# Expert rows weighted by a gate and added in memory into one row per token

## The reference, cut to what matters

```python
x = L0_attn_x                                  # 4 x 2048 x 256, so N = 8192 tokens
x = x + recurrence(layernorm(x)) * silu(ffn0(layernorm(x)))        # layer 0
xn = layernorm(x)
x = x + attention(xn) * silu(experts(xn))      # layer 1

def experts(xt):                               # E = 8, K = 2, capacity 2048
    logits = xt @ wg
    topv, topi = top_k(softmax(logits), K)
    topv = topv / sum(topv)                    # the gate
    pos, valid = place of each (token, choice) in its expert's queue, pos < capacity
    disp[topi, pos] += xt                      # rows of an expert
    y = relu(disp @ w1 + b1) @ w2 + b2         # per expert, 2048 rows
    return sum over k of gate * valid * y[topi, pos]
```

## Time and profile before

| | us |
|---|---|
| median of 3 runs | 1557.62 (1556.9 to 1558.34) |
| the profiled execution | 1556.35 |
| its span | 1554.5 |
| TensorE, VectorE busy | 1274.6, 1005.9 |
| ScalarE, GpSimd busy | 601.1, 577.3 |
| `recur` | 252.8 to 321.6 |
| `attend` | 321.6 to 659.6 |
| `route` | 659.6 to 714.6 |
| `experts` | 714.6 to 1461.75 |
| `combine` | 1461.75 to 1554.5 |

### The profile page before, as it was taken

How to read it: one execution, slowest core, us unless ns; L and a number is a source line. 1 busy time by engine, 2 the same in 40 slices (tenths; PEclk the granted TensorE clock), 3 DMA queues, 4 the chain that set the end, 5 groups by cost and what they waited for, 6 DMA issues and landing times. The chain is left out here.

```text
span 1554.5 us, 22804 instructions
## 1 busy us (share of the span) xinstructions
PE 1274.6 (82%) x7727; PEld 877.9 (56%) x7727; DVE 1005.9 (65%) x1760; ACT 601.1 (39%) x883; POOL 577.3 (37%) x540
## 2 busy tenths in 40 slices
PE   2999997769899988345999999999999999999200
PEld 1656653338777777223766666677567656766200
DVE  2788873047999999697655556555555655565297
ACT  0555553212222222102455344544544454454263
POOL 2122220003666666702333433434343333433245
PEclk9999997669999999655999999999999999999655
DMA  8000004500000000012213131221313122222596
GB/s 299 1 0 0 0 0 198 235 28 26 29 27 27 27 27 28 2 53 61 69 41 110 52 97 48 77 72 47 105 55 97 52 75 72 78 66 52 144 316 215
DMA packets 70758, 116.84 MB, mean 75 GB/s; under 512 B 6449, under 2 KB 57523, under 8 KB 68496
## 3 DMA queue, kind: packets, MB, share of 16 engines
q1 hardware_dynamic: 51456, 74.38, 14.0%
q0 software_dynamic: 12720, 33.96, 7.2%
q10 hardware_dynamic: 6496, 7.36, 1.4%
HBM read 66.13 MB, written 50.33 MB: 75 GB/s over the span
## 5 line engine op out<-in xcount | busy, mean ns | idle before, releaser
L1558 ACT ACTIVATE e_h_all<-e_pH,e_b1c,e_h_scale 128x512 f32<-128x512 f32 x256 | 199.7, 780 | 369.2 <-PE e_pH L1605 367.0
L1624 PE MATMUL e_pY<-e_w_hi,e_h_hi 128*128 128x256 f16 x1024 | 279.3, 273 | 5.0 <-DVE e_w_lo L1469 5.0
L1626 PE MATMUL e_pY<-e_w_hi,e_h_lo 128*128 128x256 f16 x1024 | 279.1, 273 | 0.0
L1625 PE MATMUL e_pY<-e_w_lo,e_h_hi 128*128 128x256 f16 x1024 | 279.1, 273 | 0.0
L1384 POOL DMA_INDIRECT e_xg<-xn_rows,e_icol x136 | 153.4, 1128 | 300.2 <-DVE e_icol L1410 258.4
L1497 DVE TENSOR_TENSOR e_h_lo<-e_h_all,e_h_hi 128x512 f16<-128x512 f32 x256 | 177.3, 693 | 107.6 <-ACT e_h_hi L1558 96.2
L1603 PE MATMUL e_pH<-e_x_hi,e_w_hi 128*128 128x512 f16 x512 | 196.4, 384 | 9.0 <-issue 6.4
L1604 PE MATMUL e_pH<-e_x_lo,e_w_hi 128*128 128x512 f16 x512 | 196.3, 383 | 0.0
L1605 PE MATMUL e_pH<-e_x_hi,e_w_lo 128*128 128x512 f16 x512 | 196.2, 383 | 0.0
L1396 POOL DMA_INDIRECT expert_rows<-e_yo,e_dcol x128 | 130.2, 1018 | 153.4 <-DVE e_yo L1521 122.4
L1521 DVE SCALAR_TENSOR_TENSOR e_yo<-e_pY,e_y_scale,logit_st 128x1024 f32<-128x1024 f32 x32 | 41.1, 1284 | 154.4 <-PE e_pY L1626 149.3
(11 more groups left out here) (226 smaller groups left out, 2293.8 us busy)
## 6 DMA issues: line engine op xcount, KB each, us to landing
raw<-expert_w SPq DMA_DIRECT2D x18, 1024.0 KB
expert_rows<-r_zero SPq DMA_DIRECT2D x16, 1024.0 KB, 15.8
xn_rows<-c_xn SPq DMA_DIRECT2D x16, 512.0 KB, 2.9
f_ya<-expert_rows SPq DMA_DIRECT2D x16, 512.0 KB, 5.2
f_yb<-expert_rows SPq DMA_DIRECT2D x16, 512.0 KB, 6.1
out<-f_ya SPq DMA_DIRECT2D x16, 512.0 KB, 3.5
x_st<-x ACTq DMA_DIRECT2D x4, 1536.0 KB, 13.9
e_xg<-xn_rows,e_icol POOLq DMA_INDIRECT x136
```

The costliest lines, as they stand in the source:

```text
L1558: last = act.activation(dst, pH[h % NPH][:, :], ACT.Relu, bias=b1c[eu][:, h:h + 1], scale=h_scale[eu][:, 0:1])
L1624: pe.matmul(pY[:, q, :], h_hi[:, h, cols], w2_hi[:, h, :], start=(h == 0), stop=False)
L1625: pe.matmul(pY[:, q, :], h_hi[:, h, cols], w2_lo[:, h, :], start=False, stop=False)
L1626: last = pe.matmul(pY[:, q, :], h_lo[:, h, cols], w2_hi[:, h, :], start=False, stop=(h == HT - 1))
```

## The change

The two rows that a token gets from its experts are weighted where they are made and added up in memory, so that the last stage reads one row per token.

- `xn_rows` gets eight more columns, the token's logits. ScalarE stores them in `attend`, one DMA per tile, at the head of the loop body (L982 of the changed file).
- The gather brings these columns along with the row. VectorE forms, after the lower half of x, the largest of the other experts' logits less this expert's own (`margin`: add a mask with -3e38 in this expert's column, maximum, subtract), ScalarE takes Exp of it, and after `yo` VectorE adds 1, takes the reciprocal, which is the gate, and multiplies the 128x1024 `yo` by it. GpSimd's scatter waits for that product.
- The scatter adds to memory (`compute_op=ALU.add`), into `expert_sums` of 8192 + 2048 rows, the last 2048 for empty places. At the end of an expert GpSimd waits until its scatters have landed, since the next expert may add to the same rows. GpSimd's loop now has four groups per iteration instead of two.
- `recur` fills 10240 instead of 16384 rows with zeros. `route` no longer makes the gates; the constants are longer by a mask and the row numbers of empty places.
- `combine` has one load, silu, product, addition and store per tile.
- In `attend` three small buffers became one, to make room; the operations are the same.

```diff
-    v.xn3_dram = nc.dram_tensor("xn3_rows", [N, D], F32, kind="Internal").ap()
-    v.y_dram = nc.dram_tensor("expert_rows", [TOPK * N, D], F32, kind="Internal").ap()
+    v.xn3_dram = nc.dram_tensor("xn3_rows", [N, D + E], F32, kind="Internal").ap()
+    v.y_dram = nc.dram_tensor("expert_sums", [N + CAP, D], F32, kind="Internal").ap()
...
-                parts = TOPK * N // (P * 8)
+                parts = (N + CAP) // (P * 8)
...
+                def store_logits(t):
+                    act.wait_ge(l_evac, t + 2)
+                    act.dma_start(rows[t][:, :, D:], v.logit_st[:, :, t, :]).then_inc(lg_out, 16)
...
-                dve.wait_ge(e_out, 1)
-                linked(dve.tensor_scalar(ep[:, :], ee[:, :], 1.0, None, ALU.add))
-                linked(dve.reciprocal(gates[:, 0, :], ep[:, :]))
-                linked(dve.tensor_tensor(gates[:, 1, :], ee[:, :], gates[:, 0, :], ALU.mult))
...
-                        pool.wait_ge(yb_ready, 2 * i + u + 1 + 1)
+                        pool.wait_ge(weighted, n + 1)
                         pool.sem_inc(passed, 1)
                         for q in range(BLK):
                             pool.indirect_dma_start(
                                 v.y_dram, bass.IndirectOffsetOnAxis(dcol[u][:, q:q + 1], axis=0), yo[u][:, q, :], None,
-                                bounds_check=TOPK * N - 1, oob_is_err=False).then_inc(y_out[u], 16)
+                                bounds_check=N + CAP - 1, oob_is_err=True, compute_op=ALU.add).then_inc(y_out[u], 16)
+                        if g == GRPS - 1:
+                            for m in range(2):
+                                pool.wait_ge(y_out[m], 8 * BLK * GRPS * (e + 1) + 16 * m)
...
+                def margin(n, u, e, first=1):
+
+                    dve.tensor_tensor(rest[:, :, :], xg[u][:, :, D:D + E], v.cst[:, C_X:C_X + (E + 1) * E][:, bass.ts(e, E)]
+                                      .unsqueeze(1).broadcast_to([P, BLK, E]), ALU.add).then_inc(gate_step, 1)
+                    dve.wait_ge(gate_step, first)
+                    dve.tensor_reduce(over[:, :], rest[:, :, :], AX.X, ALU.max).then_inc(gate_step, 1)
+                    dve.wait_ge(gate_step, first + 1)
+                    dve.tensor_tensor(gate[u][:, :], over[:, :], xg[u][:, :, D:][:, :, bass.ds(e, 1)]
+                                      .rearrange("p q o -> p (q o)"), ALU.subtract).then_inc(gate_in, 1)
...
                     x_lower(n + 1)
+                    margin(n + 1, 1 - u, e + (g + 1) // GRPS, 4 * n + 3)
                     take_icol(n + 2, u)
...
+                    dve.wait_ge(gate_out, n + 1)
+                    dve.tensor_scalar(gate[u][:, :], gate[u][:, :], 3e38, 1.0, ALU.min, ALU.add).then_inc(gate_step, 1)
+                    dve.wait_ge(gate_step, 4 * n + 5)
+                    dve.reciprocal(gate[u][:, :], gate[u][:, :]).then_inc(gate_step, 1)
+                    dve.wait_ge(gate_step, 4 * n + 6)
+                    dve.sem_inc(passed, 1)
+                    dve.wait_ge(yb_ready, n + 2)
+                    dve.tensor_tensor(yo[u][:, :, :], yo[u][:, :, :],
+                                      gate[u][:, :].unsqueeze(2).broadcast_to([P, BLK, D]),
+                                      ALU.mult).then_inc(weighted, 1)
...
                     x_upper(n + 1)
+                    margin_exp(n + 1, 1 - u)
...
-                    for k, y in enumerate((ya[n], yb[n])):
-                        sp.dma_start(y[:, :].rearrange("p (b d) -> p b d", b=B), rows[t, k]).then_inc(y_in[n], 16)
+                    sp.dma_start(ya[n][:, :].rearrange("p (b d) -> p b d", b=B), rows[t]).then_inc(y_in[n], 16)
```

More of the change, by code:

```diff
@@ L63 @@
 C_G = C_E + E
-C_ALL = C_G + TOPK * NG
+C_D = C_G + TOPK * NG
+C_X = C_D + P
+C_ALL = C_X + (E + 1) * E
 def constants():
@@ L76, in constants @@
     c[:, C_E:C_E + E] = np.arange(E)
-    c[:, C_G:] = np.ldexp(np.arange(P)[:, None] + float(P), np.arange(TOPK * NG)[None, :] - CODE)
+    c[:, C_G:C_D] = np.ldexp(np.arange(P)[:, None] + float(P), np.arange(TOPK * NG)[None, :] - CODE)
+    c[:, C_X:C_X + E * E] = np.where(np.eye(E), -3e38, 0.0).reshape(-1)
+    c[:, C_D:C_X] = N + np.arange(P)[:, None] + P * (np.arange(P) % (CAP // P))
     return c
@@ L820, in _ @@
                         sp.wait_ge(xn_ready, t + 1)
-                        sp.dma_start(rows[t], xn[u][:, :, :]).then_inc(xn_out[u], 16)
+                        sp.dma_start(rows[t][:, :, 0:D], xn[u][:, :, :]).then_inc(xn_out[u], 16)
                 for u in range(2):
                     sp.wait_ge(xn_out[u], 16 * NT // 2 + 16)
+                sp.wait_ge(lg_out, 16 * NT)
             @block.gpsimd
@@ L1291, in experts @@
         dcol = [sb(f"e_dcol{n}", [P, BLK], I32) for n in range(2)]
-        xg = [sb(f"e_xg{n}", [P, BLK, D]) for n in range(2)]
+        rest = sb("e_rest", [P, BLK, E])
+        over = sb("e_over", [P, BLK])
+        gate = [sb(f"e_gate{n}", [P, BLK]) for n in range(2)]
+        xg = [sb(f"e_xg{n}", [P, BLK, D + E + 1]) for n in range(2)]
         x_hi = sb("e_x_hi", [P, KD, W], F16)
@@ L1329, in experts @@
         y_out = [sem(f"e_y_out{n}") for n in range(2)]
+        gate_step = sem("e_gate_step")
+        gate_in = sem("e_gate_in")
+        gate_out = sem("e_gate_out")
+        weighted = sem("e_weighted")
         NGR = E * GRPS
@@ L1389, in _ @@
                     gather(u, u)
-                with pool.Fori(0, NGR // 2) as i:
-                    for u in range(2):
-                        gather(2 * i + u + 2, u)
-                        pool.wait_ge(yb_ready, 2 * i + u + 1 + 1)
+                with pool.Fori(0, E) as e:
+                    for g in range(GRPS):
+                        u = g % 2
+                        n = GRPS * e + g
+                        gather(n + 2, u)
+                        pool.wait_ge(weighted, n + 1)
                         pool.sem_inc(passed, 1)
@@ L1486, in _ @@
                 x_lower(0)
+                margin(0, 0, 0)
                 def body(e, eu, g, n):
@@ L1546, in _, with margin_exp @@
                 upper_w1(0, 0)
+                def margin_exp(n, u):
+                    act.wait_ge(gate_in, n + 1)
+                    act.sem_inc(passed, 1)
+                    act.activation(gate[u][:, :], gate[u][:, :], ACT.Exp).then_inc(gate_out, 1)
                 x_upper(0)
+                margin_exp(0, 0)
                 def body(e, eu, g, n):
@@ L1644, in combine @@
         ya = [sb(f"f_ya{n}", [P, B * D]) for n in range(NB)]
-        yb = [sb(f"f_yb{n}", [P, B * D]) for n in range(NB)]
         y_in = [sem(f"f_y_in{n}") for n in range(NB)]
         passed = sem("f_passed")
-        first_ready = sem("f_first_ready")
-        sum_ready = sem("f_sum_ready")
         silu_ready = sem("f_silu_ready")
@@ L1690, in _, with body @@
                     sp.wait_ge(o_out[n], 16 * (NT // NB) + 16)
+            @block.scalar
+            def _(act):
+                def body(i, n, left):
+                    act.wait_ge(y_in[n], 16 * (i + 1))
+                    act.sem_inc(passed, 1)
+                    act.activation(ya[n][:, :], ya[n][:, :], ACT.Silu).then_inc(silu_ready, 1)
+                rounds(act, body)
             @block.vector
             def _(dve):
-                def add(i, n):
-                    t = NB * i + n
-                    dve.wait_ge(y_in[n], 32 * (i + 1))
-                    dve.wait_ge(first_ready, t + 1)
-                    for b in range(B):
-                        cols = slice(b * D, (b + 1) * D)
-                        last = dve.scalar_tensor_tensor(ya[n][:, cols], yb[n][:, cols],
-                                                        v.gates[:, 1, bass.ds(b * NT + t, 1)], ya[n][:, cols],
-                                                        ALU.mult, ALU.add)
-                    last.then_inc(sum_ready, 1)
-                add(0, 0)
-                add(0, 1)
                 def body(i, n, left):
                     t = NB * i + n
-                    if left >= 2:
-                        add(i + (n + 2) // NB, (n + 2) % NB)
                     dve.wait_ge(silu_ready, t + 1)
@@ L1725, in _ @@
                 rounds(pool, body)
-            @block.scalar
-            def _(act):
-                def silu(t, n):
-                    act.wait_ge(sum_ready, t + 1)
-                    act.activation(ya[n][:, :], ya[n][:, :], ACT.Silu).then_inc(silu_ready, 1)
-                def first(i, n):
-                    t = NB * i + n
-                    act.wait_ge(y_in[n], 32 * (i + 1))
-                    act.sem_inc(passed, 1)
-                    for b in range(B):
-                        cols = slice(b * D, (b + 1) * D)
-                        last = act.activation(ya[n][:, cols], ya[n][:, cols], ACT.Copy,
-                                              scale=v.gates[:, 0, bass.ds(b * NT + t, 1)])
-                    last.then_inc(first_ready, 1)
-                first(0, 0)
-                first(0, 1)
-                first(0, 2)
```

(8 more changed lines are left out.)

37 lines of the change are left out of this document (14 added, 23 removed).

## The result

The changed kernel takes 1533.91 us (median of 4 runs, 1532.06 to 1535.58), the kernel before, run beside it, 1557.26 us (median of 4, 1555.96 to 1558.34): a ratio of 0.985, 95% interval 0.9833 to 0.9867. Forecast were 1535.4 us and a range of 1528 to 1556. The profiled executions have spans of 1532.4 and 1554.5 us, 22.1 us apart.

A forecast was written before the change was run, and what follows sets the result against it. VectorE, taking turns with GpSimd, was taken to bound the last stage, DMA right behind, and TensorE the expert stage. Terms -28.6 + 2.1 + 3.8 + 0.5 = -22.2 us gave 1535.4 us, range 1528 to 1556.

The forecast's parts named there:

- Turns in the last stage: Last stage: VectorE's product and GpSimd's addition exclude each other, at least 3.24 us a tile, 3.4 taken; -28.6 us.
- DMA as the second limit: Last stage: load and store of 1.05 MB per tile at 323 GB/s need 3.25 us, nearly equal to the turns.
- Rival 1: Last stage stays near 4.2 us a tile, equal reads and writes moving fewer bytes: -15.8 us, 1548 us; chance 0.13 with rival 4.
- rival 4: Last stage: GpSimd starved by lost turns, stores and loads bunch up; ends inside Rival 1's range, sharing its 0.13.
- The table load before the data: Start of the last stage: silu's table load, 1.28 us, has no wait of its own and fits before the data.
- Four first groups at 0.5 us: Expert stage: weighting delays TensorE by 0.5 us in four experts' first groups, +2.1 us (1 to 4.5).
- Loop turns as cover: Expert stage: three of seven first groups start a loop iteration with a 3.51 us gap that covers the weighting's excess.
- The scatter inside the loop at zero: Expert stage: the adding scatter costs nothing inside the loop; VectorE's index copy waits for it 13.0 us after its last issue.
- rival 3: Expert stage: adding scatter lands late and VectorE waits in 31 groups; at 15.5 us, 47 us more, 1582 us; chance 0.12.
- The end of the expert stage: After the last group nothing covers weighting, 1.8 us, and the longer adding DMA, 2 us: +3.8 us.
- The forecast's own range: Whole kernel: 1529 to 1545 us, chance 0.66; low from -28, high from -12.6 plus 1.5 us.

The follow-up runs named there:

- experiment 4: Four kernels: kernel before with new last stage alone 1528.06 us; changed kernel without its last addition 1519.36, addition on VectorE 1518.59; kernel before, addition on VectorE, 1541.15.
- experiment 1: Changed kernel with its 128 scatters writing instead of adding: 1532.48 us, ratio 0.984 against the kernel before.

## Why the prediction came out right, step by step

- **Turns in the last stage** (1.14 + 2.1 = 3.24 us at least, 3.4 taken): right, 3.28 measured, and shown by experiment 4. It rested on one subtraction, 3.75 - 1.67, and on 4.29 against 2.33 us. The 0.12 us too much per tile made 1.9 us. By the Trainium skill (SBUF — State Buffer, "Who interferes with whom") a VectorE operation with two SBUF inputs and a GpSimd operation that reads SBUF contend for a shared pair of ports, under an exclusive lock; the trace agrees: product 3.09 us beside additions, 1.22 without.
- **DMA as the second limit** (1.05 MB / 323 GB/s = 3.25 us): wrong. 323 GB/s was what the old stage asked for, not what the queues can do; they moved 385 GB/s when asked, and 373 in the old stage with its two loads once its addition was on VectorE. The step took a rate measured behind another bottleneck for a ceiling. The 1.02 of DMA share beside it looked like a full queue; with 385 GB/s it is 1.09. It did no harm only because both limits came out alike, and it hid that 15 us were to be had beside the change. Rival 1, with 0.13, rested on the same mistake and didn't come, nor did rival 4: the tiles took 3.28 us where rival 1 had 4.2.
- **The table load before the data**: wrong, 1.28 us. The row has it behind the load, at 1473.86. The row data itself came 4.3 us after the stage's start, and the prediction gave it 5.2, so most of this was covered by luck.
- **Four first groups at 0.5 us** (+2.1): wrong in place, nearly right in size. Away from the boundaries the product costs nothing (22.57 us with and without it); the slack after it is 0.44 us. The step counted a whole late start of 0.5 us through to TensorE. In the trace the first lower half of h does start 0.3 us later, 2.86 us after the yo operation against 2.55; yet TensorE's wait for the last w2 piece is as long as before:

```profile
1195.70 0.28 PE L1660 MATMUL e_pY<-e_w_hi,e_h_hi 128*128 128x256 f16 x1 [0.69 <-DVE e_w_lo L1474]
```

- **Loop turns as cover**: wrong, and opposite. The prediction read the 3.51 us gap after a turn as room for the weighting. It was a symptom: TensorE stood still there too. The cost of the weighting in the loop, 3.4 us against the kernel before in the two profiles and 2.5 us by the means, is there and nowhere else. The pauses show that it goes with the weighting's small instructions and their waits (6.2 us without the weighting, 7.8 without the product alone, 7.8 to 8.5 with all) and not with the scatter (8.7 with plain ones) or GpSimd's loop (7.8), and a fall of the clock adds 1.5 to 1.7 us where it comes. That the loop's +3.4 us lay near the +2.1 forecast is luck: the forecast had four other groups pay. **Open** is why small instructions on VectorE and ScalarE lengthen TensorE's pause, as its own program is unchanged. No run here tests a cause, and the doubled product, with pauses of only 6.7 us, speaks against a simple rule.
- **The scatter inside the loop at zero**: right; VectorE never waits for it, rival 3 didn't come, and plain scatters give the same 697 us. The step's estimate of the queue's time was right in kind: the plain kernel's queue is busy 7.8%, the adding one's 14.6%. Their difference, 6.8% of 1532 us, is 104 us, 3.3 us a group of 22. By the Trainium skill (Collectives: The Full Stack, "The bandwidth ceiling") a transfer that adds reads two sources and has half the rate, as measured there in collectives. If plain gathers and scatters cost alike, 128 of the 264 are 3.8%, and adding makes 10.6% of them: 2.8 times, not 2. That is an estimate; the measured shares decide, and the trace agrees in direction only.
- **The end of the expert stage** (1.8 + 2 = 3.8): 4.9 measured. The weighting is 1.7 us, right; the term of the sum that was mis-sized is the adding DMA, 3.3 us in the changed profile (issues 2.3, landing 0.9) and 3.05 by experiment 1. The prediction asked only how much longer the DMA lands. GpSimd's issues were its larger part, and they were taken from the plain row, 4.9 us.
- **The forecast's own range**: its high end, 1545 us, leaves out the 1.5 us that the text adds to it (1557.62 - 12.6 + 1.5 = 1546.5). Nothing hangs on it.

## What to carry to other kernels

Before two engines share the elementwise work of a stage, compare the helped engine's instruction with its length alone: 3.09 against 1.22 us says the helper costs more than it gives. A rate in GB/s is a ceiling only if something waits for the queues and nothing else sets the pace. A gap of many engines at the same moment is not slack: ask which of them is the bound, and what its clock does after the pause.

## What the runs showed of the hardware

- An indirect DMA with addition holds GpSimd 1.6 us for 128 rows of 1 KB against 1.0 us for a plain one; 128 of them bring 12288 packets more to the queue (25008 against 12720) for the same rows.
- The 16 DMA engines together moved 385 GB/s in a half-and-half mix of loads and stores, more than in loads alone (348 GB/s).
- In all kernels but the one with the doubled product a loop's turn cost 2.3 to 5.0 us where TensorE was the bound, against the 22.4 us of the same group with the loops written out: 1.9 to 3.1 us standing and, where the granted clock fell to 0.50, 1.5 to 1.7 us for that. Written out on three engines, three turns gave 14.2 us back.
- Pauses of equal length left the clock up in one kernel and took it down in another (2.31 and 2.30 us, 2.05 and 2.05 us).
